# Twelve loads on one queue, gates in the rows and a final sum in three stages: a fused attention, FFN and expert block on one core

## The chip, the cores and the metric

The kernel runs on 1 core of a Trainium2 chip. The metric is the device time of one execution in microseconds, lower is better; the number given for a kernel is the median of its runs. PE is TensorE, DVE is VectorE, ACT is ScalarE, POOL is GpSimd, and SP is the engine that here only starts DMAs. ACTq, SPq and POOLq are DMA issues by those engines.

## The reference, cut to what matters

Input x is [8, 512, 256] (8 batches of 512 tokens), the context [8, 64, 256]. All in float32.

```python
def reference(x, ctx, ...):
    # cross-attention: 16 heads of 64, 64 keys
    n = layernorm(x)
    q, k, v = (n @ Wq + bq) / 8, ctx @ Wk + bk, ctx @ Wv + bv
    x = x + softmax(q @ k.T) @ v @ Wo + bo
    n = layernorm(x)
    # dense path: 16 heads of 16, causal, then a gated FFN of 1024
    o = causal_attention(n @ wq, n @ wk, n @ wv)
    h = n + rmsnorm(o @ wo, attn_norm_w)
    dense = h + rmsnorm(silu(h @ w1) * (h @ w3) @ w2, ff_norm_w)
    # sparse path: 8 experts of 256, the best 2 of a token
    probs = softmax(n @ router_w)
    topw, topi = top_k(probs, 2)
    eo[e] = silu(n @ ew1[e]) * (n @ ew3[e]) @ ew2[e]
    moe = rmsnorm(sum_k topw[k] * eo[topi[k]], moe_norm_w)
    return x + dense + moe
```

## The kernel before

A batch of 512 tokens is four tiles of 128 rows. Every engine has its own program; all of them walk one hand-written list of steps, `STEPS`, and run the steps that concern them in its order. `walked(b, c)` gives the list in which batch b's front (cross-attention, projections, routing, row maxima of the causal scores) stands beside batch c = b − 1's back (scores, values, output, FFN). The walks are (0, none), then seven times (b, b − 1), then (none, 7); after these come the expert tiles and an ending with the FFN of batch 7 and the final sums. By the trace batch 0 takes until about 150 us, batches 1 to 7 until 1240, the last walk until 1297, the tiles until 1524, the ending until 1584.

**Replicated q and k.** The `qk` steps write three bf16 parts of q and k to a scratch tensor `parts_d` (12 stores by SP, L516, as four groups a of three; a = 0, 1 are q, counted by `q_out`, a = 2, 3 are k, counted by `k_out`). They are read back in a layout with 16 x 8 rows: six loads of 256 KB for q (`q_rep`, started by ACT in step ("v", 0), L1169) and six for k (`k_rep`, started by SP, L523). The causal products of the `max` steps (L932 and the mask L933 on PE, the reduction L1493 on DVE) need both, and stand behind the `slots` step, whose last operation is L1486 on DVE. After the loads of q, step ("v", 0) on ACT copies the batch's rows into `xk_id` (L1173), then the v copies (L1177). The `f_h_turn` step transposes h (PE L808, into PSUM), ACT copies it (L1104, `hT`), DVE keeps the rest of the rounding (L1521), and PE's FFN products `fu`, `fg` (L1011) and `fd` (L1021) of batch c follow, with ACT's tanh L1211 and DVE's L1533 and L1542.

**Start of a batch.** `CROSS` begins with m 0, m 1 (PE L835, copied by ACT L1128 and DVE L1389), then `x_turn` (L808 in two halves; the first waits for ACT's copy of m 0, the second for DVE's copy of m 1, which free the banks), then m 2, m 3. Just before, DVE has the `f_scale` step of batch c (L1578, four).

**Experts.** The `route` steps on DVE find the two best experts and their weights (`gate_b`, then a copy into `gate_all`, L1465). `scatter` on POOL writes each row twice to `xs_d`, as `xn_id` and `xk_id`: 256 values and one id that says where in `pair_d` the result goes. The expert tiles (72 of 128 rows, four per round of a loop, `in_tiles`) load rows (SP L481), transpose them (PE L1038, ACT L1241), multiply (L1047; tanh ACT L1256, DVE L1595 and L1599), transpose and copy (L1055, DVE L1588), multiply again (L1064), copy (ACT L1247), and POOL writes the rows to `pair_d` by their ids (L741, L746, L758). 72 is the number of full tiles, 64, plus one partly filled tile for each of 8 experts.

**Ending.** `ending()` lists, for m = 0 to 8, the FFN step m of batch 7 and the sum of block n: `gate` (ACT L1218, four: the first of a pair times its weight), `mix` (DVE L1548, four: the second times its weight, added), `mix_sq` (ACT L1226, four squares with sums; POOL L722 and L724 make the root), `mix_y` (DVE L1554, four: times root and norm weight; L1560 adds the dense part), and SP stores the block (L570).

## Time and profile before

| | us |
|---|---|
| median of 3 runs | 1589.32 |
| lowest, highest | 1587.12, 1589.41 |
| profiled execution, own time | 1586.43 |
| its span in the profile | 1584.7 |
| mean granted TensorE clock | 0.962 |

| engine | busy us | share of the span |
|---|---|---|
| PE | 1419.1 | 90% |
| DVE | 807.8 | 51% |
| ACT | 572.0 | 36% |
| POOL | 470.5 | 30% |

A timeline row gives the start, the length, the engine with its line, what it writes and reads, and in brackets the idle time before it with what ended it. PEclk is the clock that TensorE was granted: 1.00 is 2.4 GHz, 0.50 is 1.2 GHz, and a value between is a mean over the window.

### The profile page before, as it was taken

To read this page: it belongs to the slowest core of one execution; us is meant where nothing else is said; L and a number is where in the kernel's file an instruction comes from. 1 tells how busy PE (TensorE), PEld (TensorE's weight loads), DVE (VectorE), ACT (ScalarE), POOL (GpSimd) and SP (SyncE) were. 2 spreads that over 40 slices of the span, in tenths; PEclk is the share of its full clock that TensorE was granted. 3 is DMA by queue.
4 is the path that set the end of the run, shared out by engine and by line. 5 is a ranking of instruction groups with operands and counts; after the bars stand their busy time and mean duration, and the time that the engine had idled before them with its cause. 6 is when DMAs were issued, how large, how long until landed. Compare 5 with 4: busy or idle time off the path is not lost.

```text
span 1584.7 us, 23070 instructions
## 1 busy us (share of the span) xinstructions
PE 1419.1 (90%) x7753; PEld 933.0 (59%) x7754; DVE 807.8 (51%) x1711; ACT 572.0 (36%) x1217; POOL 470.5 (30%) x663
## 2 busy tenths in 40 slices
PE   6877898999899988998999899899989779999994
PEld 5533566656565666566656665576557436666663
DVE  2626444844484358435753674266527613333348
ACT  2231543054315421541254125413540433333344
POOL 4312122231323232213223222322232114555533
PEclk9988899999999999999999999999999989999997
DMA  5063005000600060006001500240022423432254
GB/s 200 1 186 132 17 1 146 28 15 1 149 25 15 1 160 21 9 13 158 18 1 38 136 16 1 72 102 16 1 88 59 145 83 120 128 97 86 85 203 147
DMA packets 89242, 115.62 MB, mean 73 GB/s; under 512 B 24872, under 2 KB 66368, under 8 KB 88128
## 3 DMA queue, kind: packets, MB, share of 16 engines
q1 hardware_dynamic: 73408, 79.78, 17.6%
q10 hardware_dynamic: 9216, 16.78, 3.5%
q0 software_dynamic: 6528, 17.87, 3.2%
q8 instruction: 56, 0.92, 0.2%
q14 instruction: 34, 0.28, 0.1%
HBM read 70.31 MB, written 43.68 MB: 72 GB/s over the span
## 4 chain that ended last, share of the span: by engine, by line
PE 72%; DVE 15%; ACT 4%; issue 3%; DMA 2%; ACTq 2%; POOL 1%; SPq 0%; DVEq 0%; POOLq 0%
PE ps L1011 11%; PE ps L1047 8%; PE ps L865 7%; PE ps L884 7%; PE ps L971 5%; DVE nm L1493 5%; PE ps L957 4%; PE ps L1064 4%; PE ps L932 4%; PE ps L1021 3%; PE ps L898 2%; PE ps L854 2%; ACTq L1169 2%; PE ps L991 2%; PE ps L821 2%
## 5 line engine op out<-in xcount | busy, mean ns | idle before, releaser
L1011 PE MATMUL ps<-hT,w 128*128 128x512 f32 x768 | 222.3, 437 | 30.5 <-DVE hT L1521 30.5
L1187 ACT ACTIVATE room<-ps 128x512 f32<-128x512 f32 x320 | 181.1, 598 | 159.8 <-PE ps L959 158.8
L1493 DVE TENSOR_REDUCE nm<-ps 128x2 f32<-128x256 f32 (+3 forms) x256 | 202.4, 819 | 64.0 <-PE ps L933 61.5
L1011 PEld LDWEIGHTS ps<-hT,w 128*128 128x128 f32 x768 | 152.8, 207 | 67.7 <-DVE hT L1521 33.4
L932 PE MATMUL ps<-room 96*128 96x128 bf16 (+3 forms) x512 | 125.8, 308 | 20.7 <-DVE nm L1493 15.8
L1211 ACT ACTIVATE room<-ps 128x512 f32<-128x512 f32 x64 | 38.2, 597 | 293.1 <-PE ps L1011 293.1
L1021 PE MATMUL ps<-w,room 128*128 128x256 f32 x512 | 135.2, 394 | 8.2 <-DVE room L1542 8.2
L1047 PE MATMUL ps<-room 128*128 x288 | 139.0, 605 | 1.7 <-ACT room L1241 1.7
L957 PE MATMUL ps<-room 99*128 99x384 bf16 (+3 forms) x512 | 126.0, 304 | 7.0 <-ACT room L1187 5.9
L884 PE MATMUL ps<-room 128*128 128x256 f32 x512 | 124.9, 388 | 1.9 <-ACT room L1148 1.8
L865 PE MATMUL ps<-room,xnT 128*128 128x512 f32 x256 | 123.7, 608 | 0.0
L688 POOL TENSOR_TENSOR room<-room,crec 128x1024 f32<-128x1024 f32 x32 | 60.8, 1901 | 179.1 <-DVE crec L1409 179.1
L884 PEld LDWEIGHTS ps<-room 128*128 128x128 f32 x512 | 92.6, 190 | 29.9 <-issue 14.0
L1021 PEld LDWEIGHTS ps<-w,room 128*128 128x128 f32 x512 | 90.8, 192 | 22.8 <-DVE room L1542 10.3
L933 PE MATMUL ps<-mask_qk,ident_b 128*128 128x128 bf16 x512 | 103.2, 223 | 0.0
L932 PEld LDWEIGHTS ps<-room 96*128 96x128 bf16 x512 | 50.1, 99 | 81.7 <-DVE nm L1493 42.5
L1398 DVE TENSOR_TENSOR room<-ps,room 128x1024 f32<-128x1024 f32 x32 | 39.1, 1222 | 114.3 <-PE ps L865 114.3
L1588 DVE COPY room<-ps 128x256 f32<-128x256 f32 x72 | 30.6, 424 | 130.1 <-PE ps L1055 128.1
L959 PE MATMUL ps<-mask_kq,ident_b 128*128 128x128 bf16 x512 | 96.9, 221 | 0.0
L971 PE MATMUL ps<-room,v_aug 128*32 128x512 f32 (+3 forms) x1024 | 89.7, 445 | 6.5 <-ACT room L1187 6.5
L631 POOL TENSOR_TENSOR spare_p<-neg_half 128x1 f32<-128x1 f32 x96 | 18.5, 192 | 244.3 <-DVE room L1486 160.1
L758 POOL DMA_INDIRECT pair_d<-room,ids_u x72 | 72.2, 1003 | 34.4 <-issue 32.1
(232 smaller groups left out, 2385.8 us busy)
## 6 DMA issues: line engine op xcount, KB each, us to landing
room<-parts_d ACTq DMA_DIRECT2D x48, 256.0 KB, 5.1
room<-parts_d SPq DMA_DIRECT2D x48, 256.0 KB, 5.0
room<-xs_d SPq DMA_DIRECT2D x72, 128.5 KB, 2.1
parts_d<-room SPq DMA_DIRECT2D x64, 128.0 KB, 1.8
room<-pair_d SPq DMA_DIRECT2D x8, 1024.0 KB, 7.2
room<-in_L_ffn_ew SPq DMA_DIRECT2D x24, 256.0 KB, 5.1
xin<-in_x SPq DMA_DIRECT2D x8, 512.0 KB, 7.2
parts_d<-xnT SPq DMA_DIRECT2D x32, 128.0 KB, 1.8
```

Source lines behind the costliest of these rows:

```text
L865: last = mm(bank(half), xnT[:, k, t * P:(t + 1) * P], m_sb[:, k, half * 512:(half + 1) * 512], start=(k == 0), stop=(k == KD - 1))
L884: last = mm(bank(3, D), pT[:, t % 2, a * P:(a + 1) * P], vw[:, a, :], start=(a == 0), stop=(a == PAIRS - 1))
L932: mm(bank(o, n), q_rep[0:KREP, rep_at(h), t * P:n], k_rep[0:KREP, rep_at(h), 0:n], start=True, stop=False)
L933: last = mm(bank(o, P, t * P), ident_b[:, :], mask_qk[:, :], start=False, stop=True)
L957: mm(ps[:, o:o + S - kb * P], k_rep[0:KREP + MROWS, h, kb * P:(kb + 1) * P], q_rep[0:KREP + MROWS, h, kb * P:S], start=True, stop=False, s ...
L959: last = mm(ps[:, o:o + P], ident_b[:, :], mask_kq[:, :], start=False, stop=True, skip_group_check=True)
L971: last = mm(ps[32 * j:32 * j + 32, 4 * 512 + kb * P:5 * 512], v_aug[:, v_at(kb, 4 * grp + j):v_at(kb, 4 * grp + j) + 32], prob[:, at:at + ...
L1011: last = mm(bank(up_banks(b, m)[i]), w[:, x, k, m * P:(m + 1) * P], hT[:, y, k, :], start=((x, y, k) == terms[0]), stop=((x, y, k) == term ...
L1021: last = mm(bank((6, 7)[half], D, t % 2 * D), gT[:, m % 2, t * P:(t + 1) * P], w2[:, m, :], start=(m == 0 and t % 2 == 0), stop=(m == FB - ...
L1047: last = mm(bank(2 + i % 2), xsT[:, i % 2, k * P:(k + 1) * P], ew[:, bass.ds(at + k * 2 * D, 2 * D)], start=(k == 0), stop=(k == KD - 1))
L1187: done(fn(prob[:, u * 512:(u + 1) * 512], bank(6 + n % 2), ACT.Exp), "b_exp")
L1493: done(v.tensor_reduce(nm[:, t, 2 * hp:2 * hp + 2], pair_ps, AX.X, ALU.max, negate=True), "a_max")
```

## The change

It has six parts. (1) The six loads of q move from ACT to SP, behind the twelve stores and ahead of the six loads of k. (2) `x_turn` is split: its second half stands behind m 2 and m 3. (3) `f_h_turn` of batch 7 leaves the last walk and stands in the first round of the expert tiles, on PE behind the first products of the second tile. (4) The `route` steps write the weights into the rows themselves (column D + 1 of `xn_id` and `xk_id`; with k = 1 DVE waits for the copy into `xk_id`), rows are scattered and loaded with 258 values, POOL copies a tile's column into `gates`, ACT multiplies by it in its last copy (and waits for it, as SP does before it loads over it); the copy L1465 is gone. (5) The ending has no `gate` step; `mix` is one addition on DVE over the whole block, `mix_sq` follows in the same m, a new step `by_ri` (four scalings on ACT) comes a block later, and `mix_y` (one product by the norm weight, one addition) another block later. (6) There are 71 tiles; the last round has three, and SP's last round stands outside its loop.

```diff
-MT = 2 * S * B // P + E
+MT = 2 * S * B // P + E - 1
+ROUNDS, LAST = MT // 4 + 1, MT % 4
...
-    ("m", 0), ("m", 1), ("x_turn",), ("m", 2), ("m", 3), ("shift", 1), ("bqk", 0), ("bqk", 1), ("f_hb",),
+    ("m", 0), ("m", 1), ("x_turn", 0), ("m", 2), ("m", 3), ("x_turn", 1), ("shift", 1), ("bqk", 0), ("bqk", 1), ("f_hb",),
...
-            order += [("fd", m - 1, 0), ("fd", m - 1, 1), ("gate", m - 1), ("mix", m - 1)]
+            order += [("fd", m - 1, 0), ("fd", m - 1, 1), ("mix", m - 1), ("mix_sq", m - 1)]
         if m >= 2:
-            order += [("mix_sq", m - 2), ("mix_y", m - 2)]
-    order += [("mix_sq", B - 1), ("mix_y", B - 1)]
+            order += [("by_ri", m - 2)]
+        if m >= 3:
+            order += [("mix_y", m - 3)]
+    order += [("by_ri", B - 1), ("mix_y", B - 2), ("mix_y", B - 1)]
...
@@ SP, batch
+                    need(sp, b, "q_out", per["q_out"])
+                    for j in range(NREP):
+                        src = parts_d[Q_PART[j], 0, :, :, :].rearrange("(h d) a n -> d h (a n)", d=HD)
+                        done(sp.dma_start(q_rep[j:KREP:NREP, :, :].rearrange("d (h a) n -> d h (a n)", a=KD), src), "rep_q", 16)
                     need(sp, b, "k_out", per["k_out"])
...
@@ POOL, tiles
                     g.tensor_tensor(ids_u[:, i:i + 1], xs[:, i, D:D + 1].bitcast(mybir.dt.uint32), ids_off[:, i:i + 1], ALU.add).then_inc(moe["ids"], 1)
+                    g.tensor_copy(gates[:, i:i + 1], xs[:, i, D + 1:D + 2]).then_inc(moe["gate"], 1)
...
@@ PE, tiles
                     up(t, i)
+                    if is_first and i == 1:
+                        batch(None, B - 1, only=[("f_h_turn",)])
...
@@ ACT, step ("v", 0)
-                            if c is not None:
-                                need(act, c, "b_ps", per["b_ps"])
-                            need(act, b, "q_out", per["q_out"])
-                            for j in range(NREP):
-                                src = parts_d[Q_PART[j], 0, :, :, :].rearrange("(h d) a n -> d h (a n)", d=HD)
-                                done(act.dma_start(q_rep[j:KREP:NREP, :, :].rearrange("d (h a) n -> d h (a n)", a=KD), src), "rep_q", 16)
                             need(act, b, "xn2", T)
...
@@ ACT, ending
-                    elif kind == "gate":
+                    elif kind == "by_ri":
                         n = step[1]
-                        act.wait_ge(got[n % PBUF], 16 * (n // PBUF + 1))
-                        if n >= PBUF:
-                            act.wait_ge(fin["y"], n - PBUF + 1)
+                        act.wait_ge(fin["ri"], n + 1)
                         for t in range(T):
-                            last = fn(mixed[:, n % PBUF, t, :], pair[:, n % PBUF, t, 0, :], ACT.Copy, scale=gate_all[:, n * 2 * T + 2 * t:n * 2 * T + 2 * t + 1])
-                        last.then_inc(fin["gated"], 1)
+                            last = fn(mixed[:, n % PBUF, t, :], mixed[:, n % PBUF, t, :], ACT.Copy, scale=ri_e[:, n % PBUF, t:t + 1])
+                        last.then_inc(fin["by_ri"], 1)
...
@@ ACT, tiles
+                    act.wait_ge(moe["gate"], t + 1)
+                    fn(eo[:, i, :], bank(6 + i % 2, D), ACT.Copy, scale=gates[:, i:i + 1]).then_inc(moe["eo"], 1)
...
@@ DVE, route and ending
+                            if k:
+                                need(dve, b, "xk", 1)
+                            gate = (xn_id, xk_id)[k][:, :, D + 1]
+                            link(v.tensor_reduce(gate, probs, AX.X, ALU.max))
...
-                        for t in range(T):
-                            at = n * 2 * T + 2 * t + 1
-                            last = v.scalar_tensor_tensor(mixed[:, n % PBUF, t, :], pair[:, n % PBUF, t, 1, :], gate_all[:, at:at + 1], mixed[:, n % PBUF, t, :], ALU.mult, ALU.add)
-                        last.then_inc(fin["mix"], 1)
+                        v.tensor_tensor(mixed[:, n % PBUF, :, :], pair[:, n % PBUF, :, 0, :], pair[:, n % PBUF, :, 1, :], ALU.add).then_inc(fin["mix"], 1)
                     elif kind == "mix_y":
                         n = step[1]
-                        dve.wait_ge(fin["ri"], n + 1)
-                        for t in range(T):
-                            last = v.scalar_tensor_tensor(mixed[:, n % PBUF, t, :], mixed[:, n % PBUF, t, :], ri_e[:, n % PBUF, t:t + 1], mw_bc[:, :], ALU.mult, ALU.mult)
-                        last.then_inc(fin["scaled"], 1)
+                        dve.wait_ge(fin["by_ri"], n + 1)
+                        v.tensor_tensor(mixed[:, n % PBUF, :, :], mixed[:, n % PBUF, :, :], mw_bc[:, :].unsqueeze(1).to_broadcast([P, T, D]), ALU.mult).then_inc(fin["scaled"], 1)
```

How the orders moved, at three places. A row is an instruction with its line, operation and tiles; the number ahead is its place on its engine. SP in the walks, from the last stores of the parts (`parts_d`; L516 before, L520 after) to the load of the next x, before the change:

```order
42 L516 DMA parts_d<-xnT 128x512
43 L516 DMA parts_d<-room 128x512 x2
44 L523 DMA room<-parts_d 16x8x1024 x6
45 L444 DMA room<-kt_d 64x8x64 x2
46 L444 DMA room<-vt_d 64x8x64 x2
47 L437 DMA xin<-in_x 128x4x256
```

SP at the same place after it:

```order
43 L520 DMA parts_d<-xnT 128x512
44 L520 DMA parts_d<-room 128x512 x2
45 L527 DMA room<-parts_d 16x8x1024 x6
46 L531 DMA room<-parts_d 16x8x1024 x6
47 L447 DMA room<-kt_d 64x8x64 x2
48 L447 DMA room<-vt_d 64x8x64 x2
49 L440 DMA xin<-in_x 128x4x256
```

The six loads of q (L527) stand between the stores and the loads of k (L531), on the queue that also carries the stores. ACT at that place, from its last part of k to the exponential of the routing, before:

```order
116 L1160 ACTIVATE room<-xin 128x512
117 L1169 DMA room<-parts_d 16x8x1024 x6
118 L1173 ACTIVATE room<-xn_id 128x4x256
119 L1177 ACTIVATE v_aug<-ps 128x16x16 x2
120 L1104 ACTIVATE hT<-ps 128x2x256 x2
121 L1177 ACTIVATE v_aug<-ps 128x16x16 x2
122 L1180 ACTIVATE small<-small 128x32
```

ACT there after:

```order
117 L1173 ACTIVATE room<-xin 128x512
118 L1180 ACTIVATE room<-xn_id 128x4x256
119 L1184 ACTIVATE v_aug<-ps 128x16x16 x2
120 L1117 ACTIVATE hT<-ps 128x2x256 x2
121 L1184 ACTIVATE v_aug<-ps 128x16x16 x2
122 L1187 ACTIVATE small<-small 128x32
```

The copy into `xk_id` (L1173; L1180 after) follows the part (L1160; L1173 after) with nothing between. PE at the start of a batch, from m 0 and m 1 to the first products of `bqk` (L844), before:

```order
520 L835 MATMUL ps<-room 128x128 x8
521 L808 MATMUL ps<-ident,room 128x128 x8
522 L835 MATMUL ps<-room 128x128 x8
523 L942 MATMUL ps<-ident_b,nparts 128x128 x4
524 L844 MATMUL ps<-room 128x128 x4
```

PE there after:

```order
173 L846 MATMUL ps<-room 128x128 x8
174 L819 MATMUL ps<-ident,room 128x128 x4
175 L846 MATMUL ps<-room 128x128 x8
176 L819 MATMUL ps<-ident,room 128x128 x4
177 L953 MATMUL ps<-ident_b,nparts 128x128 x4
178 L855 MATMUL ps<-room 128x128 x4
```

`x_turn` (L808; L819 after) is cut in two, with m 2 and m 3 between the halves. ACT in the ending, from its first two tanh (L1211; L1218 after) on, before:

```order
559 L1211 ACTIVATE room<-ps 128x512 x2
560 L1218 ACTIVATE room<-room,gate_all 128x256 x4
561 L1211 ACTIVATE room<-ps 128x512
562 L1218 ACTIVATE room<-room,gate_all 128x256 x4
563 L1226 ACTIVATE room,ss_e<-room 128x256 x4
564 L1211 ACTIVATE room<-ps 128x512
565 L1218 ACTIVATE room<-room,gate_all 128x256 x4
```

ACT there after:

```order
556 L1218 ACTIVATE room<-ps 128x512 x2
557 L1231 ACTIVATE room,ss_e<-room 128x256 x4
558 L1218 ACTIVATE room<-ps 128x512
559 L1231 ACTIVATE room,ss_e<-room 128x256 x4
560 L1223 ACTIVATE room<-room,ri_e 128x256 x4
561 L1218 ACTIVATE room<-ps 128x512
```

The gates (L1218) ahead of each block's squares (L1226) are gone; the squares (L1231) stand a block earlier, and behind them the scalings `by_ri` (L1223), ahead of the next tanh.

## Rows read from the trace of the kernel before

**Rows 1.** The page: the chain that ended last, by engine, shares of the span.
```profile
PE 72%; DVE 15%; ACT 4%; issue 3%; DMA 2%; ACTq 2%; POOL 1%; SPq 0%; DVEq 0%; POOLq 0%
```

**Rows 2.** Waits of PE, then ACT, whole span: us in total, times, longest.
```profile
PE ps L1011 <- DVE hT L1521: 30.5, 7, 4.4
PE ps L808 <- DVE room L1389: 11.8, 8, 1.8
...
ACT room L1173 <- issue: 35.0, 8, 4.4
```

**Rows 3.** Timeline, 1022 to 1047 us: start us, us, work, idle before, releaser.
```profile
1022.37 3.87 ACTq L1169 DMA_DIRECT2D room<-parts_d  x6
...
1025.06 1.31 SPq L516 DMA_DIRECT2D parts_d<-room  x2
...
1026.37 1.06 ACT L1173 ACTIVATE room<-xn_id 128x1024 f32<-128x1024 f32 x1 [4.34 <-issue]
...
1028.49 1.29 DVE L1521 TENSOR_TENSOR hT<-ps,hT 128x512 fp32r<-128x512 f32 x2 [6.62 <-ACT hT L1104]
...
1029.83 2.50 PE L1011 MATMUL ps<-hT,w 128*128 128x512 f32 x5 [4.33 <-DVE hT L1521]
...
1046.48 0.23 PE L932 MATMUL ps<-room 96*128 96x128 bf16 x1 [0.38 <-DVE room L1486]
```

**Rows 4.** Windows: length, busy us by engine, PEclk, DMA share, GB per second.
```profile
1029.80:1036.00 6.20, 6.17 (x15) 4.86 (x16) 1.77 (x6) 1.37 (x4) 0.00 (x0) 0.53 0.64 173
1032.00:1033.00 1.00, 1.00 (x4) 0.71 (x4) 0.00 (x0) 0.20 (x1) 0.00 (x0) 0.50 0.00 0
1036.00:1038.00 2.00, 2.00 (x10) 1.60 (x9) 1.71 (x10) 0.60 (x1) 0.00 (x0) 1.00 1.06 221
```

**Rows 5.** Line L523 (loads of k), 1020 to 1050 us: durations ns, starts, landing.
```profile
L523 SPq DMA_DIRECT2D room<-parts_d x6: 594/601/644, 1031.9 to 1035.2; - x6
...
DMA to landing us min/median/max: 3.6/5.0/6.4
```

**Rows 6.** Timeline, PE in batch 0, 89 to 103 us.
```profile
89.41 3.60 PE L821 MATMUL ps<-room 128*128 128x512 f32 x8
...
97.19 5.24 PE L821 MATMUL ps<-room 128*128 128x512 f32 x8 [3.29 <-ACT hb L1114]
```

**Rows 7.** Timeline, PE, 1091 to 1094 us.
```profile
1091.56 0.63 PE L808 MATMUL ps<-ident,room 128*128 128x128 f32 x4 [1.64 <-DVE room L1389]
...
1092.02 1.95 PE L835 MATMUL ps<-room 128*128 128x128 f32 x16
```

**Rows 8.** Timeline, PE entering the expert tiles, 1294 to 1304 us.
```profile
1294.05 2.34 PE L808 MATMUL ps<-ident,hb 128*128 128x128 f32 x8 [4.68 <-POOL hb L703]
...
1297.44 3.78 PE L1047 MATMUL ps<-room 128*128 x4 [0.62 <-ACT room L1241]
...
1302.20 1.98 PE L1047 MATMUL ps<-room 128*128 x4 [0.56 <-ACT room L1241]
```

**Rows 9.** Expert tiles, 1300 to 1500 us: window, lines (busy us, mean ns).
```profile
1300.00:1500.00 200.00, 198.88 (x777) 120.06 (x776) 75.91 (x195) 73.87 (x194) 98.45 (x250) 1.00 0.33 101
...
L1256 ACT ACTIVATE room<-ps 128x256 f32<-128x256 f32 x66 | 25.3, 383 | 92.3 <-PE ps L1047 92.3
```

**Rows 10.** Final stage, lines of 1536 to 1559 us: busy us, mean ns.
```profile
L1218 ACT ACTIVATE room<-room,gate_all 128x256 f32<-128x256 f32 x18 | 7.7, 498 | 0.0
L1226 ACT ACTIVATE room<-room 128x256 f32<-128x256 f32 x19 | 7.7, 406 | 5.2 <-DVE room L1548 5.2
...
L1548 DVE SCALAR_TENSOR_TENSOR room<-room,gate_all 128x256 f32<-128x256 f32 x16 | 6.7, 477 | 0.0
...
L1560 DVE TENSOR_TENSOR room<-room 128x1024 f32<-128x1024 f32 x4 | 4.9, 1226 | 0.1
...
L1211 ACT ACTIVATE room<-ps 128x512 f32<-128x512 f32 x5 | 3.0, 590 | 0.5 <-PE ps L1011 0.5
L1542 DVE SCALAR_TENSOR_TENSOR room<-room,ps 128x512 f32<-128x512 f32 x4 | 2.7, 686 | 0.1
```

More of the change, by code:

```diff
@@ L505, in experts_first, with batch @@
                 tiles(0, True, False)
-            def batch(b, c, end=False):
+            def batch(b, c, end=False, only=None):
                 if c is not None:
@@ L631, in carry_wait, with batch @@
                 g.tensor_tensor(spare_p[:, i:i + 1], neg_half[:, 0:1], neg_half[:, 0:1], ALU.mult)
-            def batch(b, c, end=False):
+            def batch(b, c, end=False, only=None):
                 steps = {"pool_a": 0, "pool_f": 1 if end else 0}
@@ L646, in crossed @@
                     rsqrt(b, rs2[:, t:t + 1], mv2[:, t, 1:2], 0, "rstd2", "pool_a", ve_a)
-                for step in walked(b, c, end):
+                for step in only or walked(b, c, end):
                     if step[0] in ("x_stats", "nx_stats"):
@@ L654, in batch @@
                         done(g.tensor_tensor(rs1[:, :], ve_n[:, :], neg_half[:, :], ALU.pow), "rstd1")
-                    elif step[0] == "x_turn" and (c is None or c == 0):
+                    elif step == ("x_turn", 0) and (c is None or c == 0):
                         if c is None:
@@ L750, in tiles @@
                     row_ids(1, 1, 0)
-                for i in range(4):
+                for i in range(LAST if is_last else 4):
                     t = q * 4 + i
-                    if not (is_last and i >= 2):
+                    if not (is_last and i >= LAST - 2):
                         row_ids(t + 2, (i + 2) % 4, q + (i + 2) // 4)
@@ L794, in _, with batch @@
             pe.wait_ge(p0["const"], 9)
-            pe.wait_ge(p0["iota"], 3)
+            pe.wait_ge(p0["iota"], 4)
             def v_at(kb, h):
                 return (kb * H + h) * (HD + 1)
-            def batch(b, c, end=False):
+            def batch(b, c, end=False, only=None):
                 def turn(n, src, banks, waits, name, halves=(0, 1)):
@@ L809, in turn @@
                         done(last, name)
-                for step in walked(b, c, end):
+                for step in only or walked(b, c, end):
                     kind = step[0]
@@ L1098, in _, with batch @@
                     fn(wqT[:, a0:a0 + 4, k * P:(k + 1) * P], src.rearrange("p (a n) -> p a n", a=4), ACT.Copy).then_inc(p0["tr_sb"], 1)
-            def batch(b, c, end=False):
+            def batch(b, c, end=False, only=None):
                 def spread(n, dst, banks, src_name, name, halves=(0, 1)):
@@ L1104, in spread @@
                         done(fn(dst[:, :, t2 * 2 * P:(t2 + 1) * 2 * P], bank(banks[t2]).rearrange("p (k n) -> p k n", k=KD), ACT.Copy), name)
-                for step in walked(b, c, end):
+                for step in only or walked(b, c, end):
                     kind = step[0]
@@ L1256, in tiles @@
                     fn(e_th[:, i % 2, :], bank(2 + i % 2, D), ACT.Tanh, scale=0.5).then_inc(moe["th"], 1)
-                    if not (is_last and i == 3):
+                    if is_first and i == 1:
+                        batch(None, B - 1, only=[("f_h_turn",)])
+                    if not (is_last and i == LAST - 1):
                         x_out(t + 1, i + 1)
@@ L1343, in make_table, with batch @@
                 v.tensor_scalar(spare_off[:, :], start, float(P), None, ALU.mult).then_inc(moe["table"], 1)
-            def batch(b, c, end=False):
+            def batch(b, c, end=False, only=None):
                 links = [0]
@@ L1365, in normed @@
                     done(v.tensor_scalar(xn[:, t, :], x1[:, t, :], mv2[:, t, 0:1], rs2[:, t:t + 1], ALU.subtract, ALU.mult), "xn2")
-                for step in walked(b, c, end):
+                for step in only or walked(b, c, end):
                     kind = step[0]
@@ L1588, in g_out @@
                     v.tensor_copy(e_gT[:, i % 2, :], bank(4 + i % 2, D)).then_inc(moe["gT"], 1)
-                for i in range(4):
+                for i in range(LAST if is_last else 4):
                     t = q * 4 + i
+                    if is_first and i == 1:
+                        batch(None, B - 1, only=[("f_h_turn",)])
                     if not (is_first and i == 0):
@@ L1600, in tiles @@
                 if is_last:
-                    g_out(t, 3)
+                    g_out(t, LAST - 1)
             in_tiles(dve, tiles)
```

68 lines of the change are left out of this document (35 added, 33 removed).

## The prediction

> **What bounds the kernel now.** I read the page's chain first: PE makes 72% of the work that ended last, DVE 15% [rows 1]. So time goes out only where PE has no work or runs at half clock, and in the two stages where DVE sets the pace. I then read the waits by engine, which name the recurring stops of PE, and what ended them: 30.5 us in 7 waits before L1011, 11.8 us in 8 before L808, and on ACT 35.0 us in 8 waits that nothing but its own issuing explains [rows 2]. Each of these belongs to one place per batch, so I read one batch (1010 to 1092 us) by its timeline, the clock and the DMA share by windows, then the entry to the expert tiles, the tiles, and the final stage.
>
> **Part 1, the loads of q (batches 1 to 7).** ACT issues six loads in 3.87 us from 1022.37, then makes the copy L1173, which stood ready behind them (4.34 idle), and only then the copies of hT. DVE's L1521 follows, and PE starts L1011 at 1029.83 after 4.33 us of nothing [rows 3]. After that stop the granted clock is 0.53 in the mean from 1029.8 to 1036 [rows 4]: 0.47 x 6.2 = 2.9 us of work lost too. Without the issues L1173 starts 4.34 us earlier, and all that follows it on ACT and DVE with it, but for 0.15 us in which hT's copy now waits for its transposes: L1011 starts 4.2 us earlier, at full clock, and PE would reach the first score product (L932) 4.2 + 2.9 = 7.1 us earlier, at 1039.4 or so. The slots (L1486), which ended its wait before [rows 3], hang on the same products and would be done by 1039.7.
> But L932 also needs the replicated q and k. SP's last two stores of the parts are issued from 1025.06 on for 1.31 us [rows 3], half a microsecond less once no other loads are being started beside them (an estimate); the six q loads would follow from 1025.8 and the six k loads right behind, since stores no longer wait beside loads. Of the k loads the first, issued at 1031.9, lands 3.6 us later and the sixth, issued at 1035.2, 6.4 us later: 1035.5 and 1041.6, five steps of 1.2 us for 256 KB each [rows 5]. The DMA engines' share is 1.06 meanwhile, so this is transfer and not issuing, while at 1032 to 1033 they lay at 0.00, SP waiting for the stores [rows 4]. First landing 1025.8 + 3.6 = 1029.4, twelfth 1029.4 + 11 x 1.2 = 1042.6. So L932 starts at about 1042.7 in place of 1046.48: **3.8 us for each batch, 7 x 3.75 = 26.3 us**, and a new wait of PE of about 3.1 us appears before L932. The kv and x loads that stand behind them on SP come a microsecond later than now and are not wanted for 30 us: nothing.
> What does the new wait do to the clock? PE's waits of 4.33 and 3.29 us were each followed by half clock [rows 3, 4, 6]; behind the 1.64 of x_turn sixteen L835 take their 1.95 us as at full clock [rows 7]. After 3.29 us eight L821 took 5.24 us where they take 3.60 at full clock [rows 6]: 1.64 lost. Bounds: 0 (as after 1.64) and 2.9 (as after 4.33). I take 1.6, by the row of nearest length: **−7 x 1.6 = −11.2 us**. The Trainium skill ("TensorE: Matmul & The Clock Gate", What's actually happening) says that the gate's default is throttled and that it closes after an idle stretch it has watched as a whole; by that page a wait of about this length may pass unseen in some batches, which would leave part of the 11.2 in hand, as rival 1 has it.
> **Batch 0.** The same issues hold ACT for 4.4 us [rows 2], and PE stands 3.29 us before L821 and loses 1.64 behind it [rows 6]. Here slots come late enough to cover the loads: **+4.9 us** (3 to 4.9).
>
> **Part 2, x_turn split.** L808's second half waits 1.64 us for m1's copy on DVE (L1389) [rows 7], which stands in DVE's order behind the four L1578 of the batch before. Now the sixteen products of m2 and m3 (1.95 us) go between; they need only the first copies and the last maxima, both done. The cover is 1.95 against 1.64, so all of it goes: **7 x 1.6 = +11.2 us**, against 11.8 us in the 8 waits of that kind [rows 2]. Nothing is late next: m3's copy now comes right behind m1's on DVE.
>
> **Part 3, h's transposes at the end of the walk.** PE waits 4.68 us before L808 for POOL's hb (sums, root, norm, add, one after the other), then runs at half clock: up 0 takes 3.78 against 1.98 for up 1 [rows 8]. After, the first two tiles go ahead of L808. Half clock costs 1.8 in up 0, 1.1 in L808 (half of its 2.34) and by the same share some 0.6 in the transposes of the first rows: 3.5. Of the wait I leave 1.1 for the first tile's own chain (its rows' landing, two transposes, ACT's copy), an estimate: 4.68 − 1.1 + 3.5 = **+7.1 us** (5 if the clock falls all the same behind that, 7.5 if the wait is 0.7).
>
> **Parts 4 and 6, tiles.** 66 silu steps of ACT in 200 us make 3.03 us a tile, with PE busy 198.9 of 200 [rows 9]. One tile fewer: **+3.0 us**. The new copy of a gate on POOL (at most its mean operation, 98.5/250 = 0.39 us) and the scale by an operand in the copy of ACT lie beside PE: POOL is busy 98.5 of 200 us, ACT 73.9 [rows 9]. The gate's wait on ACT stands behind dn_ps, which comes 2 tiles after the row. Nothing; without the cover 0.39 x 71 = 28 us, if POOL were the limit, and it has half of its time free. The copy of the gates dropped in each route step is off PE's path.
>
> **Part 5, the final sum.** Now a block lasts 23/4 = 5.75 us (16 L1548 in 23 us), paced by DVE: two products of 0.69, two fours of 0.477 and an add of 1.23 make 6.4 by their own durations, which overlap a little at their ends, so DVE never rests [rows 10]. After, DVE has u, g, an add, a product and an add, each of the last three as L1560 (same size): 2 x 0.69 + 3 x 1.23 = 5.1, 5.0 with the overlap. But the hand-over closes a ring through ACT's order: th(m) 0.7 (0.6 as an L1211 of this size, [rows 10], and the handover), u and g 1.35, the add 1.2, four squares 1.65 that wait for it, four scalings 1.6 (between four L1226 of 0.406 and four L1218 of 0.498), then th(m+1), which stands behind them on ACT: 6.5 us. Before, ACT's gates waited for no DVE step of the same block. So from block 3 on 0.75 us more a block, less what the first blocks save: the last u comes at 1567.5, 2.9 later than now. The tail is as long as it was (squares, root on POOL, scaling on ACT, product and add on DVE, 17.5 us): **−3.2 us** (−5, or +4 if DVE alone sets the pace).
>
> **The sum.** 26.3 − 11.2 + 4.9 + 11.2 + 7.1 + 3.0 − 3.2 = 38.1 us. The profiled run took 1586.43 (span 1584.7 and 1.7 around it): 1548.3. The median of the runs lies 2.9 above the profiled one, so 1551.
>
> **Rivals.**
> 1. *The new wait costs no clock, or is short.* If the loads land at 1.1 us each the wait is 2.0 us, and the 11.2 are kept: 38.1 + 11.2, and 7 x 1.1 = 7.7 more at best, gives 1532 to 1540. For it: waits up to 1.64 us passed. Against: 3.29 did not. Chance 0.17.
> 2. *The wait costs the full 2.9, or the loads are slower.* With 2.9 a batch: 1.3 x 7 = 9.1 more, 1560. With 1.35 us a load as well (twelfth at 1044.3): another 11.6, 1572. For it: all seven waits of 4.33 cost that, and stores and loads now share one queue. Chance 0.2.
> 3. *Slower than before.* Place: L932 of each batch, waiting for the last k load, behind eleven others and the stores on SP's queue. The other terms bring 23.0 us, or 3.3 a batch; with 2.9 of clock the balance is reached when L932 starts 0.4 later than now, at 1046.9, which is 1.6 us a load. At 1.9 us a load it starts at 1050.4: 3.9 + 2.9 − 3.3 = 3.5 a batch, 24.5 us in all, 1614. For it: a load has taken up to 6.4 us to land, and both transfers move 3 MB together. Against: 1.2 us a load in either queue. By the Trainium skill ("DMA: Bandwidth & Descriptors", Issuing engines are not separate DMA queues) the queues' transfers run on the same 16 DMA engines, whoever starts them; by it the twelve would take no longer in one queue than in two, which speaks against this rival. Chance 0.04.
> 4. *The final ring doesn't close* because ACT gets ahead, and DVE sets 5.0 us a block: 7 us better, 1544. Against: the order of ACT. Chance 0.07, inside the range.
>
> **How the numbers follow.** The forecast with its own bounds (1541 to 1560) has 0.52, rival 1 0.17, rival 2 0.2, rival 4 0.07, rival 3 0.04. Range for 8 in 10: 1535 to 1567. About 0.2% (3 us) is what a measurement can tell from no change. Faster 0.94, same 0.02, slower 0.04.
>
> **What would show it.** Before L1011 (hT) ACT's wait for its own issuing and PE's 30.5 us are gone; before the first score product of a batch PE waits about 3 us for a DMA, some 21 us in all, and half clock follows; the distance from one batch to the next falls by 3.8 us (5.4 without clock loss); PE's 1.64 before x_turn's second half is gone; up 0 and up 1 of the tiles take the same time; a block of the final stage lasts 6.5 us with the end of the squares and scalings before each th. I am wrong if the last k load lands before 1041 or after 1045 on the scale of rows 3, if the clock stays up, or if another wait (DVE's route steps, now early) stands before L932.

## The result, and the profile after

The changed kernel takes 1551.47 us (median of 4 runs, 1549.08 to 1551.92) against 1589.37 (median of 4): the ratio is 0.976, 95% interval 0.974 to 0.978. The forecast was 1551, in a range of 1535 to 1567. The total came out to half a microsecond, and part of that is luck. By the medians 37.9 us went, by the profiled executions 35.1, and the sum had 38.1. The runs below show that two of its terms, priced by undoing them, were off by about 10 us each, in opposite directions.

The profiled execution took 1551.35 us, its span is 1549.6, 35.1 less than before. Set side by side by the starts of the same operations (us from the start of the span; the product is the first score product of a batch, L932 before and L943 after; the last wo is the first of the last sixteen L991, now L1002; the last up product is the last L1047, now L1058):

| stretch | before | after | less | forecast |
|---|---|---|---|---|
| start to batch 0's first score product | 119.46 | 115.18 | 4.3 | 4.9 |
| that product, batch 0 to batch 7 | 1080.57 | 1055.00 | 25.6 | 26.3, this line and the next |
| batch 7's product to the last wo | 85.62 | 87.08 | −1.5 | |
| last wo to the last up product of the tiles | 231.57 | 221.71 | 9.9 | 10.1 |
| from there to the end | 67.48 | 70.63 | −3.2 | −3.2 |

From batch 2 on, a batch (from its first m, L835 before and L846 after, to that of the next) takes 150.0 to 150.9 us where it took 153.5 to 153.7: 3.4 us less in the mean, forecast 3.8.

The waits of PE over the whole span answer to [rows 2]; the columns are us in total, times and the longest. The page's chain, for comparison with [rows 1], covers only a few per cent of the span here (it breaks at the load of a pair in the ending) and says nothing of the walks.

```profile
PE ps L943 <- DMA room<-parts_d: 30.8, 7, 5.1
PE ps L943 <- DVE nm L1502: 15.8, 44, 1.8
PE ps L1032 <- DVE room L1551: 10.4, 5, 4.4
```

The 30.5 us before the FFN products (L1011, now L1022) and the 11.8 before `x_turn` are gone, and so are ACT's 35.0 us behind its own issues. In the first's place stand 30.8 us in seven waits for a DMA before the score product: as much idle time as the stop had. What the batch gained is that the product comes earlier, and that half clock behind the wait is shorter. Batch 6 in the timeline, with the rows that answer to [rows 3] (start, length, work, idle time before it and what ended it):

```profile
998.67 1.04 ACT L1180 ACTIVATE room<-xn_id 128x1024 f32<-128x1024 f32 x1
...
1001.74 0.95 SPq L520 DMA_DIRECT2D parts_d<-room  x2
...
1002.12 5.86 PE L1022 MATMUL ps<-hT,w 128*128 128x512 f32 x24
...
1002.82 3.87 SPq L527 DMA_DIRECT2D room<-parts_d  x6
1006.72 3.82 SPq L531 DMA_DIRECT2D room<-parts_d  x6
...
1020.05 0.22 PE L943 MATMUL ps<-room 96*128 96x128 bf16 x1 [4.27 <-DMA room<-parts_d]
```

ACT's copy L1180 follows at once, and the 24 products L1022 start at 1002.12 and take 5.86 us, 0.24 each, where at half clock five had taken 2.50 [rows 3]. SP issues all twelve loads in a row from 1002.82, without a wait for the stores in between. The k loads land 7.1 to 9.9 us after their issue, where [rows 5] had 3.6 to 6.4, since six others are ahead of them (the first load of q lands 3.7 us after its issue); columns of the window are as in [rows 4]:

```profile
L531 SPq DMA_DIRECT2D room<-parts_d x6: 598/600/612, 1006.7 to 1009.9; - x6
...
DMA to landing us min/median/max: 7.1/8.5/9.9
```

```profile
1015.00:1019.90 4.90, 0.78 (x4) 0.29 (x2) 0.94 (x6) 0.60 (x1) 0.19 (x1) 1.00 1.14 199
1019.90:1024.10 4.20, 4.04 (x16) 3.01 (x17) 1.52 (x3) 0.00 (x0) 1.07 (x1) 0.59 1.04 220
```

First landing 1002.8 + 3.7 = 1006.5, last 1009.9 + 9.9 = 1019.8: eleven steps in 13.3 us, 1.21 us each, as between the loads of k in [rows 5]. While PE waits the DMA engines' share is 1.14; behind the wait the granted clock is 0.59 in the mean.

The other places. `x_turn`: its second half (L819) follows m 2 and m 3 (L846) without the 1.64 us of [rows 7].

```profile
1064.44 0.63 PE L819 MATMUL ps<-ident,room 128*128 128x128 f32 x4
1064.90 1.95 PE L846 MATMUL ps<-room 128*128 128x128 f32 x16
1066.71 0.63 PE L819 MATMUL ps<-ident,room 128*128 128x128 f32 x4
```

The entry to the tiles, against [rows 8]: 4.68 us of wait and a first tile of 3.78 have become two short waits and two tiles of 1.98, and h's transposes take 1.04 where they took 2.34.

```profile
1262.50 1.98 PE L1058 MATMUL ps<-room 128*128 x4 [0.57 <-ACT room L1246]
...
1265.31 1.98 PE L1058 MATMUL ps<-room 128*128 x4 [0.62 <-ACT room L1246]
1267.13 1.04 PE L819 MATMUL ps<-ident,hb 128*128 128x128 f32 x8
```

In the tiles, against [rows 9], PE is busy for 198.6 of 200 us and a tile takes 3.06 us (by the starts of the up products, L1058), as in the kernel before. The copy with the gate as an operand (L1253) takes 473 ns where the same copy without it (L1247 before) took 383, and waits 7.5 us in 63 tiles for the gate from POOL; PE does not wait for it.

```profile
1264.00:1464.00 200.00, 198.56 (x780) 120.29 (x779) 78.00 (x199) 80.11 (x195) 111.71 (x323) 1.00 0.32 102
...
L1253 ACT ACTIVATE room<-ps,gates 128x256 f32<-128x256 f32 x63 | 29.8, 473 | 33.8 <-PE ps L1075 26.3 <-POOL gates L757 7.5
```

The copy in the kernel before, 1300 to 1500 us:

```profile
L1247 ACT ACTIVATE room<-ps 128x256 f32<-128x256 f32 x63 | 24.1, 383 | 33.9 <-PE ps L1064 33.9
```

The ending, against [rows 10], two blocks of it on DVE and ACT: u (L1542) waits 1.46 us for the tanh (L1218), which follows the four scalings (L1223, 1.69), which follow the squares (L1231), which waited 2.61 us for the addition (L1557). From u to u it is 6.40 us; the forecast's ring was 6.5.

```profile
1504.34 1.22 DVE L1557 TENSOR_TENSOR room<-room 128x1024 f32<-128x1024 f32 x1
...
1505.59 0.42 ACT L1231 ACTIVATE room<-room 128x256 f32<-128x256 f32 x1 [2.61 <-DVE room L1557]
...
1507.20 1.69 ACT L1223 ACTIVATE room<-room,ri_e 128x256 f32<-128x256 f32 x4
...
1508.81 0.57 ACT L1218 ACTIVATE room<-ps 128x512 f32<-128x512 f32 x1
1509.41 0.69 DVE L1542 SCALAR_TENSOR_TENSOR room<-room,ps 128x512 f32<-128x512 f32 x1 [1.46 <-ACT room L1218]
...
1511.99 0.42 ACT L1231 ACTIVATE room<-room 128x256 f32<-128x256 f32 x1 [2.61 <-DVE room L1557]
```

### The profile page after: what moved, and what is told of

Read it like the earlier page. It is cut to its first block and busy times, and to the rows that moved or that the text cites. A ratio compares the mean times of both kernels' runs of the same rounds, so it can differ in the third digit from the quotient of the medians.

```text
span 1549.6 us, 23080 instructions
## 1 busy us (share of the span) xinstructions
PE 1403.3 (91%) x7741; PEld 925.4 (60%) x7742; DVE 810.6 (52%) x1652; ACT 576.5 (37%) x1214; POOL 476.7 (31%) x731
## 5 line engine op out<-in xcount | busy, mean ns | idle before, releaser
L1022 PE MATMUL ps<-hT,w 128*128 128x512 f32 x768 | 210.8, 419 | 0.0
L943 PE MATMUL ps<-room 96*128 96x128 bf16 (+3 forms) x512 | 127.9, 312 | 48.7 <-DMA room<-parts_d 30.8
L1022 PEld LDWEIGHTS ps<-hT,w 128*128 128x128 f32 x768 | 143.0, 194 | 32.6 <-DVE hT L1530 2.0
L1218 ACT ACTIVATE room<-ps 128x512 f32<-128x512 f32 x64 | 38.0, 594 | 302.6 <-PE ps L1022 302.6
L1032 PE MATMUL ps<-w,room 128*128 128x256 f32 x512 | 138.0, 400 | 10.4 <-DVE room L1551 10.4
L1058 PE MATMUL ps<-room 128*128 x284 | 135.5, 599 | 1.9 <-ACT room L1246 1.9
L943 PEld LDWEIGHTS ps<-room 96*128 96x128 bf16 x512 | 51.0, 101 | 112.2 <-issue 50.6
L968 PEld LDWEIGHTS ps<-room 99*128 99x128 bf16 x512 | 50.2, 98 | 51.9 <-ACT room L1194 20.7
```

The costliest lines, as they stand in the source:

```text
L943: mm(bank(o, n), q_rep[0:KREP, rep_at(h), t * P:n], k_rep[0:KREP, rep_at(h), 0:n], start=True, stop=False)
L968: mm(ps[:, o:o + S - kb * P], k_rep[0:KREP + MROWS, h, kb * P:(kb + 1) * P], q_rep[0:KREP + MROWS, h, kb * P:S], start=True, stop=False, s ...
L1022: last = mm(bank(up_banks(b, m)[i]), w[:, x, k, m * P:(m + 1) * P], hT[:, y, k, :], start=((x, y, k) == terms[0]), stop=((x, y, k) == term ...
L1032: last = mm(bank((6, 7)[half], D, t % 2 * D), gT[:, m % 2, t * P:(t + 1) * P], w2[:, m, :], start=(m == 0 and t % 2 == 0), stop=(m == FB - ...
L1058: last = mm(bank(2 + i % 2), xsT[:, i % 2, k * P:(k + 1) * P], ew[:, bass.ds(at + k * 2 * D, 2 * D)], start=(k == 0), stop=(k == KD - 1))
```

## The experiments

Eleven kernels ran, each a small edit of the changed kernel, all but two timed in four runs against six or seven of the kernel before. "Half clock" is a granted clock of 0.50 of full speed.

### Part 1 alone undone

```diff
@@ SP, batch
-                    need(sp, b, "q_out", per["q_out"])
-                    for j in range(NREP):
...
@@ ACT, step ("v", 0)
+                            need(act, b, "q_out", per["q_out"])
+                            for j in range(NREP):
...
```

> The changed kernel with part 1 alone undone: the six loads of q are started by ACT again, ahead of the copy into xk_id. Theory (the loads are bound by transfer, the new wait before the first score product costs its half clock): the batch loses 3.2 us before that product and gets 1.6 us of clock back, 1.6 x 7 = 11 us, and some 5 us in batch 0: 1567 (1564 to 1571), with PE's 4.3 us before the FFN products of each batch back and the wait for a DMA before the first score product gone. Rival (part 1 only exchanged one wait for another, the gain came from the other parts): 1549 to 1554. Rival (the FFN stop costs more than predicted): above 1575.

Measured: 1561.92 us (ratio to the kernel before 0.984, 0.981 to 0.986). By the median, part 1 is worth 10.4 us, not the 20 of the prediction (26.3 − 11.2 + 4.9), and the time is 2 us below the lower end expected. The four runs lie in two pairs, 1559.16 and 1559.33, 1564.50 and 1566.01, so the price is 7.7 to 14.5 us. The stop is where it was expected:

```profile
PE ps L1018 <- DVE hT L1532: 30.4, 7, 4.4
```

The clock behind it is not what it was. In this kernel half clock behind PE's stop of 4.33 us lasts 3.4 us in five of the seven batches, and 6.8 in two; in the kernel before it lasts 6.8 in all seven. Read by the starts in batch 6, from the values' product to the first score product it takes 25.74 us here, 26.75 in the kernel before and 23.58 in the changed one; from there to the next batch 40.91, 40.90 and 42.48. So part 1 brings 2.2 − 1.6 = 0.6 us a batch next to the other parts. The trace is that of the longest run, 14.6 us above the changed kernel's: 4.0 of them come before batch 0's score product, 6.4 between that and batch 1's, and 3.9 in the six batches after. What the 6.4 consist of is not resolved. The other five parts bring 25.7 us where the prediction had 18.1.

### Part 2 alone undone

```diff
-    ("m", 0), ("m", 1), ("x_turn", 0), ("m", 2), ("m", 3), ("x_turn", 1), ("shift", 1), ("bqk", 0), ("bqk", 1), ("f_hb",),
+    ("m", 0), ("m", 1), ("x_turn", 0), ("x_turn", 1), ("m", 2), ("m", 3), ("shift", 1), ("bqk", 0), ("bqk", 1), ("f_hb",),
```

> The changed kernel with part 2 alone undone: both halves of x_turn stand together again, ahead of m 2 and m 3. Theory: PE's wait of 1.6 us before the second half is back in 7 batches: 1551.5 + 11 to 13 = 1563.5. Rival (the first clock-lowering wait before it makes that stretch run longer or shorter, so that the price isn't 1.6): 1556 or less, or 1570 or more.

Measured: 1571.86 us (0.991, 0.989 to 0.993), the rival's side: part 2 is worth 20.4 us. The wait itself is the 1.65 us forecast in six of seven batches (12.2 us in 8 waits, the longest 2.2). But the clock behind the wait for the loads now stays low for longer, 6.8 us in five of the seven batches (one in the changed kernel). The waits of this kernel, and a window of 8 us around that point in batch 5, then the same window of the changed kernel:

```profile
PE ps L943 <- DMA room<-parts_d: 31.4, 7, 5.0
...
PE ps L819 <- DVE room L1397: 12.2, 8, 2.2
...
882.00:890.00 8.00, 6.70 (x26) 4.68 (x27) 2.62 (x5) 0.00 (x0) 2.03 (x2) 0.57 0.76 144
```

```profile
869.00:877.00 8.00, 7.07 (x36) 5.21 (x37) 4.19 (x6) 0.00 (x0) 2.69 (x3) 0.79 0.77 150
```

0.57 against 0.79 is 1.8 us a batch. Four more batches of it make some 7 us, the wait 11.5; 2 us are left without a place. So a part's price depends on what the clock does behind a wait that another part made, and prices by undoing one part do not add up: 10.4 and 20.4, where the prediction had 20.0 and 11.2. By the table above, the two together brought 28.4 us up to the last wo (4.3 + 25.6 − 1.5), where the forecast had 31.2. That two errors of 9 us cancel is why the total came out.

The lengths of the batches show the same. All the lengths here are from batch 2 on. In the kernel before, half clock behind the stop begins every 153.6 us, and the batches take 153.5 to 153.7. In the changed kernel half clock behind the wait begins every 150.2 us, and the batches take 150.0 to 150.9. With part 2 undone they take 151.8 to 153.6. The difference between the two kernels is as long as one short stretch of half clock, 3.4 us, and not the sum of the waits and the lost work that the forecast counted. Whether the clock's timing sets the length of a batch, or only follows it, no run here settles.

### Part 3 alone undone

```diff
-    return [("shift", 1), ("f_hb",)] + SCORES + [("out_t", G - 1), ("f_o_turn",), ("f_wo",), ("f_wo_sq",), ("f_o_norm",), ("f_yb",)]
+    return [("shift", 1), ("f_hb",)] + SCORES + [("out_t", G - 1), ("f_o_turn",), ("f_wo",), ("f_wo_sq",), ("f_o_norm",), ("f_h_turn",), ("f_yb",)]
...
@@ PE, ACT and DVE, first round of the tiles
-                    if is_first and i == 1:
-                        batch(None, B - 1, only=[("f_h_turn",)])
```

> The changed kernel with part 3 alone undone: h's transposes of the last batch stand in the last walk again, ahead of the first expert tile. Theory: PE's wait of 4.7 us for POOL's hb and the half clock behind it are back: 1551.5 + 7 = 1558.5 (1556.5 to 1559.5). Rival (the first tiles' loads would have held PE there anyway): 1551 to 1554.

Measured: 1560.07 us (0.982, 0.980 to 0.984), 8.6 more. From the last wo to the last up product it is 228.6 us against 221.7: 6.9, close to the forecast's 7.1. In the profiled execution another 3.4 us lie before batch 0's score product (118.6 us from the start against 115.2), where this edit touches nothing: that stretch takes 111.8 to 118.6 us over the kernels with part 1. The stop and the slow first tile are back:

```profile
1269.30 0.66 PE L819 MATMUL ps<-ident,hb 128*128 128x128 f32 x4 [4.69 <-POOL hb L713]
...
1272.68 3.78 PE L1058 MATMUL ps<-room 128*128 x4 [0.62 <-ACT room L1244]
```

### How long the wait is, and what the clock does behind it

Three kernels cut the last three, two or one of the six k loads of batches 1 to 7 to a corner, and so leave out the k they bring.

```diff
+                        if c is not None and j >= 3:
+                            done(sp.dma_start(k_rep[j:KREP:NREP, 0:2, :].rearrange("d (h a) n -> d h (a n)", a=KD), src[:, 0:1, :]), "rep_k", 16)
+                            continue
                         done(sp.dma_start(k_rep[j:KREP:NREP, :, :].rearrange("d (h a) n -> d h (a n)", a=KD), src), "rep_k", 16)
```

(j >= 4 and j >= 5 in the other two.)

> The changed kernel with the last three of the six k loads of batches 1 to 7 cut to a corner (2 of 128 partitions' rows), so that the k they bring is left out there; nothing else. Theory (transfer-bound, 1.2 us a load; the wait before the first score product costs its own length and 1.6 us of clock): the wait falls from 4.3 to 0.7 to 1.0 us and the clock stays up: 7 x (3.5 + 1.6) = 36 us less than the changed kernel, 1516. Rival (the clock falls there for another reason than the wait): half clock stays, 1527. Rival (issuing or a fixed latency sets the landing, not the bytes): above 1540.

> As the one before with two of the six k loads cut. Theory: the wait is 4.3 - 2.4 = 1.9 to 2.1 us in each batch. Whether half clock follows a wait of that length is what this run is for: after 1.64 it did not, after 3.3 it did. If it does: 1534, if not: 1523.

> As the one before with one of the six k loads cut, which makes the wait as long as was predicted for the changed kernel (3.1 us). Theory: half clock follows in all seven batches and costs 1.6 each: 1543. Rival (a wait of that length is passed over in part of the batches): half clock in fewer than seven, 1532 to 1541.

Measured: 1527.49 us (0.962, 0.960 to 0.964) with three cut; one run each with two cut, 1538.37, and with one cut, 1544.86. All three are longer than the theory had (1516, 1523 or 1534, 1543). 1527 was the figure of the rival by which half clock stays, but the trace does not bear that rival out: half clock followed in three of seven batches. With two cut it followed in four, with one cut in six, four of them 6.8 us long. The waits of PE with three cut:

```profile
PE ps L946 <- DMA room<-parts_d: 12.6, 7, 2.8
```

12.6 us in seven is 1.8 each, so three loads take away 2.6 us of wait and not 3.6: a cut load still costs 0.3 us (an estimate, 1.2 − 2.6/3). 24 us went, two thirds of the theory's 36. So most of the landing's time is the size of the transfer, and not all of it. In the two other kernels too the waits are longer than was meant (with two cut 2.3 to 3.7 us, meant 1.9 to 2.1; with one cut 3.1 to 4.7, meant 3.1). What the runs are worth more for is the clock. Over the eight kernels with this wait, the changed one and seven of its edits, there are 56 waits of PE for these loads, and half clock followed

| wait of PE | waits | followed by half clock |
|---|---|---|
| 1.34 to 1.55 us | 4 | 0 |
| 1.79 to 3.35 us | 13 | 8 |
| 3.45 to 5.09 us | 39 | 39 (22 of 3.4 us, 17 of 6.8) |

At two other places it is the same: twelve waits of 1.64 or 1.65 us before `x_turn` (six in the kernel before, six with part 2 undone) were not followed by half clock, and all 21 stops of 4.3 to 4.4 us before the FFN products were (the kernel before and the two kernels with q's loads on ACT). Two waits of one and the same length in the kernel with one load cut show the middle line: the first is passed over, the second is not.

```profile
1016.52 0.22 PE L946 MATMUL ps<-room 96*128 96x128 bf16 x1 [3.30 <-DMA room<-parts_d]
...
1164.11 0.22 PE L946 MATMUL ps<-room 96*128 96x128 bf16 x1 [3.30 <-DMA room<-parts_d]
```

```profile
1016.50:1020.00 3.50, 3.48 (x23) 2.69 (x24) 2.25 (x4) 0.00 (x0) 1.34 (x2) 1.00 1.19 252
1164.10:1168.70 4.60, 4.59 (x19) 3.24 (x20) 2.30 (x4) 0.00 (x0) 1.76 (x2) 0.63 0.08 29
```

1.00 behind the one, 0.63 behind the other. Behind the waits of 3.45 us and more it always fell, behind the middling ones in part; how long it stays low is not settled by the length of the wait (5.02 and 5.09 us were followed by 3.4 us, 3.07 and 3.45 by 6.8). The forecast's wait of 3.1 would have been in the middle line; the real one of 4.3 was not. The Trainium skill ("TensorE: Matmul & The Clock Gate", What's actually happening) has the gate close after an idle stretch it has watched as a whole. The first line of the table, where no wait was followed by half clock, agrees; the eight waits of 1.79 to 3.35 us that were followed by it do not, going by the figure that the page gives for that stretch, and there the measurement decides.

### Three of the q loads earlier on SP's queue

```diff
@@ SP, batch: stores of the parts
                     for a in range(4):
+                        if a == 3:
+                            if c is not None:
+                                need(sp, c, "b_ps", per["b_ps"])
+                                sp.sem_inc(freed, 1)
+                            need(sp, b, "q_out", per["q_out"])
+                            load_q(range(3))
...
+                    load_q(range(3, NREP))
```

> The changed kernel with SP starting three of the six q loads ahead of the last three stores (group a = 3) and the other three behind them. Theory (twelve loads at 1.2 us each, one behind the other, set the first score product): the first load starts some 3 us earlier, the twelfth lands some 3 us earlier, PE's wait falls from 4.3 to about 1.3 us and the clock stays up: 7 x (3.0 + 1.6) = 32 us and 1 to 3 in batch 0: 1518. Rival (the stores behind the loads land so late that the k loads start no earlier, as when SP waited for them in the kernel before): 1540 to 1551. Rival (the wait of 1.3 us is followed by half clock all the same): 1529.

Measured: 1546.76 us (0.974, 0.971 to 0.977), 4.7 less than the changed kernel, the rival's side. PE's waits are 27.1 us in seven, 3.9 each. SP's queue in batch 6:

```profile
992.65 3.06 SPq L531 DMA_DIRECT2D parts_d<-room  x2
995.84 1.93 SPq L520 DMA_DIRECT2D room<-parts_d  x3
997.81 0.59 SPq L531 DMA_DIRECT2D parts_d<-xnT  x1
...
999.39 1.86 SPq L520 DMA_DIRECT2D room<-parts_d  x3
1002.74 3.77 SPq L536 DMA_DIRECT2D room<-parts_d  x6
...
DMA to landing us min/median/max: 4.9/6.2/8.1
```

The last store of group a = 2 comes late in L531 x2 from 992.65 (it waits for POOL), so the first load goes out at 995.84, only 1.5 us earlier than it would have by the changed order. The stores of a = 3 now lie among the loads, and SP waits for them before the k loads (1001.3 to 1002.74). The last k load lands 8.1 us behind its issue at 1005.9, at 1014.0: 0.2 us earlier against the batch's own start than in the changed kernel. From 1000 us to that landing the DMA engines' share is 1.06 to 1.13. So starting earlier does not end earlier here: the same twelve loads and three stores, 3.4 MB, have to be moved, only in another order.

### FFN block 3 ahead of the first max step

```diff
-for _m in range(3, FB):
...
+STEPS += [("fu", 3, 0), ("fg", 3, 0), ("fu", 3, 1), ("fg", 3, 1), ("fd", 2, 0), ("fd", 2, 1)]
+for _m in range(4, FB):
+    _c = (0, 2, 4, 6, 8) if _m < 6 else (0, 1, 2, 4, 6)
...
```

> The changed kernel with FFN block 3 (fu, fg, fd) of the batch before wholly ahead of the first max step, and the 32 max steps spread over the other four blocks. PE then has about 4.8 us of work while the loads of q and k land. Theory (the wait of 4.3 us is pure waiting for the transfer, followed by half clock for 1.6 us): the wait falls under 0.5, the clock stays up, and if the stretch of the max steps stays bound by PE, 5.9 x 7 = 41 us go: 1510. Rival (the stretch of the max steps becomes bound by DVE, whose reductions have less PE work beside them): half of that is given back, 1525 to 1535. Rival (the wait was worth nothing): 1551.

Measured: 1517.17 us (0.956, 0.953 to 0.958), 34.3 less than the changed kernel, 4.9 a batch. In five of the seven batches PE's work now reaches to the landing of the loads and the score product follows it with 0.1 us of idle time or none; in the other two it still waits 0.9 and 1.1 us for them. In batch 6:

```profile
993.24 1.75 PE L1024 MATMUL ps<-hT,w 128*128 128x512 f32 x6
994.84 0.23 PE L945 MATMUL ps<-room 96*128 96x128 bf16 x1
...
PE ps L945 <- DVE nm L1504: 20.1, 44, 1.8
```

```profile
994.80:1031.70 36.90, 33.92 (x216) 23.58 (x215) 32.44 (x58) 3.96 (x12) 10.38 (x13) 1.00 0.20 52
```

```profile
1020.00:1062.50 42.50, 40.12 (x234) 27.98 (x234) 33.77 (x60) 3.96 (x12) 10.37 (x13) 0.96 0.17 45
```

The last two fences are windows over the stretch of the max steps, of this kernel and of the changed one. It has become 5.6 us shorter, since a block of the FFN has left it; PE is 92% busy and DVE 88%. The rival's bound is near, and PE's waits for DVE's reductions have grown from 15.8 to 20.1 us, which is 0.6 a batch. In none of the seven batches does half clock follow there. The forecast of 1510 was 7 too low; 4 of it are those waits for DVE, 2 the two waits for the loads, and 1 has no place.

### The same order with q's loads on ACT

> FFN block 3 ahead of the first max step as in e2_fill, and the six loads of q started by ACT as in the kernel before. With this order the new wait has other work before it, so this prices the moved loads where nothing takes their gain back. Theory (part 1 is worth the 4.3 us stop of PE and its half clock, 1.7 to 2.9, in seven batches, and 5 us in batch 0): 1517.2 + 7 x 6.0 to 7.2 + 5 = 1564 to 1572. Rival (most of the gain of e2_fill would come without part 1, since k's loads on SP then land 1.3 us earlier against the maxima): under 1550.

Measured: 1562.37 us (0.983, 0.981 to 0.986), 2 us below the range expected. It is 45.2 us above the kernel with the loads on SP, and just what the older order gave with the loads on ACT (1561.92). So the new order brings nothing without part 1, and part 1 brings 10 us without the new order and 45 with it. The stop is back, one per batch:

```profile
PE ps L1020 <- DVE hT L1534: 30.5, 7, 4.4
```

### by_ri ahead of the squares in the ending

```diff
-            order += [("fd", m - 1, 0), ("fd", m - 1, 1), ("mix", m - 1), ("mix_sq", m - 1)]
+            order += [("fd", m - 1, 0), ("fd", m - 1, 1), ("mix", m - 1)]
         if m >= 2:
             order += [("by_ri", m - 2)]
+        if m >= 1:
+            order += [("mix_sq", m - 1)]
```

> The changed kernel with by_ri(m-2) ahead of mix_sq(m-1) on ACT in the ending, nothing else. Theory (the block of 6.4 us is a ring th, u, g, mix, four squares, four scalings, next th): the scalings then run while DVE does u, g and mix, the block falls to 5.0 to 5.1 us, DVE's own work, and five blocks bring 6.5 to 7 us: 1544.5. Rival (DVE or PE sets the block, not the ring): 1551, no change.

Measured: 1547.18 us (0.976, 0.973 to 0.980), 4.3 less. The runs' spread (1546.11 to 1554.12) alone would not bear this out, but the trace does: from the ending's first FFN product to the end of the span it is 61.1 us against 65.8. DVE's rows in two blocks:

```profile
1505.81 0.68 DVE L1544 SCALAR_TENSOR_TENSOR room<-room,ps 128x512 f32<-128x512 f32 x1
...
1509.51 1.23 DVE L1568 TENSOR_TENSOR room<-room 128x1024 f32<-128x1024 f32 x1
1510.88 0.69 DVE L1544 SCALAR_TENSOR_TENSOR room<-room,ps 128x512 f32<-128x512 f32 x1
...
1515.74 0.68 DVE L1544 SCALAR_TENSOR_TENSOR room<-room,ps 128x512 f32<-128x512 f32 x1
...
1534.92 1.23 DVE L1563 TENSOR_TENSOR room<-room,mw_bc 128x1024 f32<-128x1024 f32 x1 [2.91 <-ACT room L1225]
```

From u to u it is 5.07 and 4.86 us, and DVE hardly rests: the ring was real, and DVE's own work is what stands below it. Of the 7 us expected 2 were given back at the end, where DVE's last product by the norm weight waits 2.91 us for the scaling of block 7 (in the changed kernel the only such wait was 0.98).

### Both orders together

> The changed kernel with both orders moved: FFN block 3 ahead of the first max step, and by_ri ahead of mix_sq in the ending. They lie in different stages and should add up: 1517.2 - 4.3 = 1513 (1511 to 1515). Rival (the ending's gain is the clock's phase and not the ring): 1517.

Measured: 1508.67 us (0.950, 0.948 to 0.952), 8.5 less than with the first order alone, and 2 below the range expected (1511 to 1515). The ending brings what it did alone (61.0 us from its first FFN product to the end, 66.0 with the first order alone). The rest lies ahead of it, where this edit changes nothing, and stays unexplained. It is the fastest kernel here, 2.8% below the changed one.

## Why the prediction was right

**Part 1.** The mechanism stood: the stop before the FFN products goes, PE reaches the score product 7 us earlier and waits for the twelfth load. With batch 6 shifted by 23.26 us, so that the values' product starts at the same time as before, the loads start at 1026.1 (forecast 1025.8), the first lands at 1029.8 (1029.4), the twelfth at 1043.1 (1042.6) and the product starts at 1043.3 (1042.7): 3.2 us a batch in place of 3.75, 22 us in seven and not 26.3. What was mis-sized: 0.25 us from the landing to the product was left out, 0.3 at the start, and PE was ready at 1039.0, so that the wait was 4.3 and not 3.1 (3.3 by the forecast's own 1042.7 and 1039.4).

**The clock behind the new wait.** 1.6 us a batch was taken and 1.58 measured in batch 6. That is luck: the row it came from was of a wait of 3.29 us, and the wait here was 4.27. And the step treated the clock as a price of this one wait. The runs show that half clock lasts 3.4 or 6.8 us behind a stop, and which of the two it is changes with the other parts: 6.8 in all seven batches before, in two with part 1 undone, in five with part 2 undone, in one of the changed kernel. That shifted some 9 us from part 1 to part 2.

**Batch 0**: from the values' product to the score product it takes 25.4 us where it took 30.9, so part 1 brought 5.5 there (4.9 forecast); to the start of the program the difference is 4.3. **Part 2**: the wait of 1.65 us went as forecast and nothing came in its place, but undoing it cost 20.4 and not 11.2 us, some 7 of the difference by the clock as above. **Part 3**: 6.9 by the trace, 7.1 forecast. **Part 6**: 3.0, as forecast. **Part 4**: nothing for PE, as forecast. The scaling copy on ACT got 0.09 us a tile slower, for which the forecast had no price, and it does wait for the gate (7.5 us in 63 tiles), where the forecast had it covered; both lie beside PE. **Part 5**: −3.15 against −3.2, with a block of 6.40 against 6.5, and the kernel with the other order confirms the ring.

**The total.** Up to the last wo 28.4 us went and 31.2 were forecast; the tiles and the ending came to within 0.3. That makes the 35.1 of the profiled executions against 38.1. The forecast then added 2.9 us, because the kernel before had been profiled in an execution that much below its median; the changed kernel's profiled execution lies at its median. So two misses of 3 us cancelled, and the half microsecond is no measure of the sum.

**Rivals.** Rival 1 needed a wait short enough to be passed over; none of the seven, 4.1 to 5.1 us long, was. The longer half clock of rival 2 (6.8 us) stood behind one wait of seven. Rival 3's loads of 1.6 us did not come: the twelve took 1.21 us each in one queue, and the six of k had taken 1.2 when q's came from another. The Trainium skill ("DMA: Bandwidth & Descriptors", Issuing engines are not separate DMA queues) says that DMAs run on the same 16 engines whoever starts them; the trace agrees. Rival 4 fell with the ring.

## What to carry to other kernels

When an edit removes a stop of the busiest engine, look at once for the transfer that was hidden behind it, and give the engine other work up to its landing: here moving the loads was worth 10 us without that work and 45 with it, and the new place of that work was worth nothing without the moved loads. When one engine's queue carries both the issue of loads and copies that others wait for, move the loads. A total that comes out is no proof of its terms: undo the parts one by one.

## What the runs showed of the hardware

Before the first score product, half clock followed none of four waits of PE up to 1.55 us, eight of thirteen between 1.79 and 3.35, and all of 39 from 3.45 on; it then lasted 3.4 or 6.8 us, whatever the length of the wait. A Copy on ACT of 128x256 with a scale taken from a tile took 473 ns against 383 without it (L1253 and, before, L1247; from PSUM in both). Twelve loads of 256 KB in rows of 2 KB, on one queue, landed 1.21 us apart in the mean (batch 6).
